# Two-layer kernel: triangular inverse in place on GpSimd, Gram with one stationary, and spreads in four row groups at once

## The chip, the cores and the metric

One core of a Trainium2 chip runs the whole program in one launch. The metric is the device time of that core in microseconds, the median over runs. TensorE (PE, with its weight loads PEld), VectorE (DVE), ScalarE (ACT) and GpSimd (POOL) run side by side and meet at semaphores; SyncE (SP) issues the plain DMAs.

## What is computed

Two transformer-like layers on x of shape 4 x 1024 x 256, all in fp32, each with adaptive shift, scale and gate per batch. Only layer 0 and the start of layer 1 touch the change.

```
layer 0, mixer:  k, q, v = short_conv(x @ W + b);  beta = sigmoid(x @ Wbeta)
                 delta rule, 16 heads of 16, per time step:
                 S += beta * k (v - k S);   o = q S
                 out = rmsnorm(o) @ Wo
layer 0, ffn:    16 routed experts of 64 channels, the best 2 per token by softmax,
                 weights renormalised; 2 shared experts of 128 channels
                 y = sum_e weight_e * (silu(x Wg_e) * (x Wu_e)) Wd_e + shared
layer 1, mixer:  complex gated linear recurrence h = a h + k v, 8 heads of 32; y = q h
layer 1, ffn:    8 experts of 1024 channels, top 2 per token
```

The delta rule is computed in chunks of 32 steps. Within a chunk it needs the inverse of a unit triangular 32 x 32 matrix for each of 16 heads x 4 batches x 4 chunks: 256 such matrices a segment, two on each of the 128 partitions.

## The kernel before, in words

**Segments.** Time is cut into eight segments of 128 steps (with 4 batches, 512 tokens). `turn(seg, rest, nxt, pre)` is called on every engine for seg = -2 to 7 and writes out each engine's order by hand. `rest` (0 to 7) is the main work of the segment, `nxt` (-1 to 6) is the delta rule of the next segment, `pre` (-2 to 5) projections, convolutions and keys of the one after. An engine runs its instructions in the order written, so a wait holds up all behind it. After the segments the experts of layer 1 run, then a last mix; the change does not touch these.

**The inverse.** At the start of a turn TensorE forms the Gram matrices (`gram`, L1959): for each head pair, batch and chunk one 32 x 32 stationary of keys Kc against beta-scaled keys of even and odd heads (EXP[0:2], 64 columns, L1966) and one stationary of scaled keys KpT against the queries (EXP[2:4], L1970). VectorE masks them into NA (L1273), SP writes NA[0] out to n_d and reads it back transposed across partitions (L584, L589), which raises n_in. Then GpSimd and VectorE take turns: for t = 1 to 31 and two halves c, GpSimd multiplies the t x t part found so far with row t (`products`, L1754, instruction L1761) and VectorE sums each row of the product into column t of Usub (`substitute`, L1187, instruction L1193), 62 of each a turn. VectorE's share is cut into pieces, `SUB_STEPS = (1, 8, 13, 16, 18, 20, 22, 24, 26)` and `SUB_LATE = 29`: one piece after each routed tile of the ffn, one before the down residuals, one after the norm, and t = 29 to 31 in the middle of layer 1's first scores, after L1479 and before L1484. sub_ok lets SP write Usub out to u_d and back into NA (L596, L601), for TensorE's `delta_rows` (L1980) late in the turn. In turn -1 the two engines do this with no other work on them.

**The expert tiles of layer 0** (TensorE from L2082, VectorE `hidden_tile`, L1328): ten tiles of 128 channels, the first two shared. A tile is four matmuls of 128x512 (gate into bank 3(i%2), up into the next bank; an fp32 matmul stands in the profile as two records). ScalarE takes silu of the gate (L809), VectorE multiplies with up (L1333), and for routed tiles with the token's routing weights (L1337). These have to stand on the right channels: VectorE makes the 16 weights of a token (L1362), TensorE turns them (`turn_weights`, L2079), VectorE copies them (L1364), and `spread(i)` (L2074) multiplies the 16 x 512 weights with a 16 x 128 selection matrix. TensorE turns and spreads tiles 2 and 3 only before tile 4; from tile 4 on, each spread stands behind its own tile. The gate of tile i waits for hid0_ok of tile i-2. Ten down matmuls a batch follow (L2108), residual and norm on VectorE (L1375 to L1392).

**Layer 1's first scores.** After twelve plane matmuls, `level(0, 0)` (L2182) scores batch by batch and puts `value_columns(b)` behind each: a bias matmul of one row (ones x b_v, L2135) that opens the bank, and two value matmuls (L2137). `level(1, 0)` needs the values taken by ScalarE. GpSimd zeroes the near scores and Hx (L1771 to L1774), multiplies for t = 29 to 31, waits for sub_ok, and zeroes score (L1780) and, after the values, the ring's score halves (L1784). VectorE's take (L1421) needs the third zeroing.

**Keys on ScalarE.** `spread_queries` (L780) copies the queries once for even and once for odd heads; then come the squares of the output (L1013), then `take_scaled_keys(k)` (L786, L788), three copies of a bank each: KpT and the two of EXP[0:2].

## Time and profile before

| | |
|---|---|
| median of 3 runs | 3630.91 us (3629.87 to 3631.79) |
| the profiled execution's own time | 3636.34 us |
| its span | 3634.4 us |
| mean granted TensorE clock | 0.817 |
| busy: TensorE, VectorE, ScalarE, GpSimd | 2796.7, 2038.2, 1163.9, 660.7 us |
| first GpSimd product of the turns -1 to 6 | 158.9, 334.7, 671.2, 1007.8, 1344.5, 1683.2, 2019.9, 2354.7 us |

The profile is one execution. A timeline row gives start, duration, engine, line, operation, output and inputs, shape and count of merged instructions, and in brackets the idle time before them with what ended it ("issue": nothing that the profile shows). The chain of waits follows the work that ended last back to the start. The granted clock is the share of TensorE's full clock, 1.00 or 0.50.

### The profile page before, as it was taken

What the parts mean: (1) busy time and instruction counts of PE and PEld (TensorE: products, weight loads), DVE (VectorE), ACT (ScalarE), POOL (GpSimd) and SP (SyncE); (2) the same over time, 40 slices, a digit from 0 to 9 for tenths busy, and PEclk for the clock granted to TensorE, in tenths of its full rate; (3) what the DMA queues carried; (4) which work ended last, traced back from release to release, by engine and by line L of the source; (5) the groups of instructions that cost most, each with busy time, mean ns of one, the idle gap of its engine ahead of it and who ended that gap; (6) DMA issues with size and microseconds to landing.
All of it is one profiled execution on the core that took longest, in us unless ns stands there. A gap on an engine that the chain in (4) does not pass through costs nothing.

```text
span 3634.4 us, 82025 instructions
## 1 busy us (share of the span) xinstructions
PE 2796.7 (77%) x35840; PEld 2039.6 (56%) x35840; DVE 2038.2 (56%) x4528; ACT 1163.9 (32%) x2276; POOL 660.7 (18%) x682
## 2 busy tenths in 40 slices
PE   3438869977896888699768978895787639999990
PEld 3225457545645664565457446645544538888880
DVE  4445785687669567955776596679336630000004
ACT  0212354145424433432353235325223512222210
POOL 0231500430051016004300510160001000000006
PEclk8667977988796879688976978796788769999995
DMA  2122201310121121112201311211110035565645
GB/s 84 24 59 42 53 8 43 78 34 24 44 58 31 42 49 46 19 43 65 48 2 55 70 31 43 48 36 25 42 41 19 2 117 193 196 198 186 200 160 166
DMA packets 230023, 247.57 MB, mean 68 GB/s; under 512 B 147361, under 2 KB 187169, under 8 KB 227361
## 3 DMA queue, kind: packets, MB, share of 16 engines
q1 hardware_dynamic: 223520, 225.54, 21.4%
q0 software_dynamic: 6144, 16.79, 1.5%
q8 instruction: 282, 4.62, 0.5%
q14 instruction: 77, 0.62, 0.1%
HBM read 196.15 MB, written 46.14 MB: 67 GB/s over the span
## 4 chain that ended last, share of the span: by engine, by line
PE 57%; DVE 21%; ACT 7%; POOL 4%; issue 4%; DMA 1%; SPq 0%; POOLq 0%; DVEq 0%
PE banks L1874 17%; PE banks L2391 7%; PE banks L2410 7%; PE banks L2108 4%; POOL arena L1761 3%; PE banks L2202 2%; PE banks L2207 2%; PE banks L1884 2%; POOL arena L1814 2%; PE banks L2182 2%; PE banks L1980 1%; PE banks L1948 1%; PE banks L2074 1%; PE banks L2021 1%; DVE arena L1523 1%
## 5 line engine op out<-in xcount | busy, mean ns | idle before, releaser
L1761 POOL TENSOR_TENSOR arena<-arena 128x1 f32<-128x1 f32 (+30 forms) x496 | 443.0, 921 | 726.4 <-DMA arena<-n_d 430.1
L1791 POOL DMA_INDIRECT h_d<-h_tok,pos_now x64 | 65.9, 1030 | 1499.0 <-DVE pos_now L1626 1482.0
L2182 PE MATMUL banks<-arena 32*32 32x64 f32 (+2 forms) x6144 | 208.7, 322 | 164.1 <-DVE arena L1526 91.7
L1193 DVE TENSOR_REDUCE arena<-arena 128x1 f32<-128x1 f32 (+30 forms) x496 | 243.1, 502 | 162.9 <-POOL arena L1761 158.3
L1874 PE MATMUL banks<-hT,ring 128*128 128x512 f32 x640 | 314.9, 645 | 8.8 <-DVE arena L1337 8.1
L2182 PE MATMUL banks<-arena,xn 32*32 32x64 f32 (+2 forms) x6144 | 193.0, 314 | 154.4 <-DVE xn L1526 117.8
L2182 PEld LDWEIGHTS banks<-arena 32*32 32x32 f32 (+2 forms) x6144 | 186.0, 196 | 204.8 <-DVE arena L1526 114.4
L1045 ACT ACTIVATE arena<-banks,arena 128x256 f32<-128x256 f32 x312 | 130.7, 470 | 457.1 <-PE banks L2391 457.1
L2391 PE MATMUL banks<-arena 128*128 128x256 f32 x1248 | 276.9, 381 | 0.0
L2410 PE MATMUL banks<-arena 128*128 128x256 f32 x1248 | 275.7, 379 | 0.0
L2182 PEld LDWEIGHTS banks<-arena,xn 32*32 32x32 f32 (+2 forms) x6144 | 177.4, 192 | 175.1 <-DVE xn L1526 128.7
L926 ACT ACTIVATE arena<-banks 32x512 f32<-32x512 f32 (+1 forms) x288 | 169.2, 588 | 290.7 <-PE banks L2182 224.4
L2391 PEld LDWEIGHTS banks<-arena 128*128 128x128 f32 x1248 | 238.3, 191 | 32.6 <-issue 0.4
L2410 PEld LDWEIGHTS banks<-arena 128*128 128x128 f32 x1248 | 234.6, 190 | 30.0
L1874 PEld LDWEIGHTS banks<-hT,ring 128*128 128x128 f32 x640 | 126.8, 205 | 187.8 <-issue 186.9
L1874 PE MATMUL banks<-arena,ring 128*128 128x512 f32 x512 | 224.0, 596 | 6.2 <-ACT arena L827 6.2
L1706 DVE COPY arena<-banks 128x512 f32<-128x512 f32 x39 | 27.0, 692 | 271.4 <-PE banks L2379 271.4
L1814 POOL DMA_INDIRECT arena<-y_d,y_at x64 | 64.6, 1009 | 609.5 <-DMA y_d<-arena 590.3
L1874 PEld LDWEIGHTS banks<-arena,ring 128*128 128x128 f32 x512 | 96.1, 190 | 128.2 <-issue 112.8
L1716 DVE TENSOR_TENSOR arena<-banks,arena 128x512 f32<-128x512 f32 x39 | 27.0, 692 | 249.4 <-PE banks L2410 249.4
L809 ACT ACTIVATE arena<-banks 128x512 f32<-128x512 f32 x80 | 47.8, 597 | 314.0 <-PE banks L1874 314.0
L2108 PE MATMUL banks<-ring,arena 128*128 128x256 f32 x640 | 140.8, 381 | 0.6 <-DVE arena L1337 0.6
(352 smaller groups left out, 5106.1 us busy)
## 6 DMA issues: line engine op xcount, KB each, us to landing
arena<-in_w_ring SPq DMA_DIRECT2D x78, 1024.0 KB, 5.1
ring<-in_w_ring SPq DMA_DIRECT2D x104, 512.0 KB, 4.5
arena<-h_d SPq DMA_DIRECT2D x39, 256.0 KB, 5.3
y_d<-arena SPq DMA_DIRECT2D x39, 256.0 KB, 5.8
n_d<-NA SPq DMA_DIRECT2D x8, 1024.0 KB, 3.8
arena<-n_d SPq DMA_DIRECT2D x16, 512.0 KB, 7.8
u_d<-arena SPq DMA_DIRECT2D x8, 1024.0 KB, 4.6
NA<-u_d SPq DMA_DIRECT2D x32, 256.0 KB, 6.5
```

The lines of the kernel that those rows point to most:

```text
L926: ins_ = act.activation(laid_, made, ACT.Copy)
L1045: ins_ = act.activation(hid1[:, i % 2, t], bank[pair][:, half * T1:(half + 1) * T1], ACT.Gelu, bias=b1[:, i % 2, t:t + 1])
L1193: dve.tensor_reduce(Usub[:, c, 0:t, t], part, AX.X, ALU.add).then_inc(*up(sub_sum, me))
L1761: pool.tensor_tensor(part, Usub[:, c, 0:t, 0:t], Nsub[:, c, t, 0:t].unsqueeze(1).to_broadcast([P, t, t]), ALU.mult)\
L1814: pool.indirect_dma_start(out=y_of[:, s % 3, k, b], out_offset=None, in_=y_d, in_offset=spot)\
L1874: i_ = mm(dst, w[:, k, cols_], rhs(src, k), start=(k == 0), stop=(k == n - 1))
L1884: i_ = mm(bank[banks[j]][:, i * D:(i + 1) * D], src[:, k, 2 * j + i, :], w[:, k, :], start=(k == 0), stop=(k == KC - 1))
L2108: i_ = mm(bank[DOWN_BANKS[b]][:, 0:D], hid0[:, i, b, :], downs[d][:, i - first, :], start=(i == 0), stop=(i == TILES0 - 1))
L2182: i_ = mm(bank[4 * hg + h][keys, b * width:(b + 1) * width], K2[rows_, r, b, keys], q, start=(r == 0), stop=(r == 1), skip_group_check=True)
L2202: mm(y, Hx[:, b, r, 2 * j:2 * j + 2].rearrange("p h j -> p (h j)"), Q3[:, 1 + r, b, :], start=(r == 0), stop=False, skip_group_check=True)
L2391: i_ = mm(bank[t // 2][:, (t % 2) * T1:(t % 2 + 1) * T1], w1[:, i % 2, t // 4, at_:at_ + P], h_cols[:, i % 2, k], start=(k == 0), stop=(k ...
L2410: i_ = mm(bank[4 + i % 2][:, j * D:(j + 1) * D], hid1[:, i % 2, t, j * P:(j + 1) * P], w2[:, i % 2, t // 4, t % 4 * D:(t % 4 + 1) * D], st ...
```

## The change

It makes five edits.

- The inverse is computed in place by outer products: Usub is loaded with the strictly triangular matrix, the diagonal is set to one, and for s = 1 to 30 the part right of s of the rows above s gains column s times row s. That is one multiply of 2 x s x (31-s) elements into sub_prod and one add of the same size, each waiting for the one before, 60 in all and a memset. In segments 0 to 6 all of it is GpSimd's, from n_in on and ahead of its zeroing; in turn -1 all of it is VectorE's. VectorE's pieces between the tiles, after the norm and within the scores are gone. Nsub and two memsets at the start are gone.
- The Gram matrices have one stationary: KpT against unscaled keys and queries together, 128 columns. The mask is turned over to suit the transposed result.
- ScalarE's EXP[0:2] come from Kc in SBUF (`spread_keys`, four copies directly behind `spread_queries`) and no longer from the banks in `take_scaled_keys`.
- The routing weights are written eight times over (comb_wide) and turned into all 128 partitions, between gate and up of tile 3; then four spreads, one in each group of 32 rows, run for tiles 2 to 5 before tile 4 and for tiles 6 to 9 before tile 7, into banks of their own. The selection matrix is loaded at four bases.
- The four value bias matmuls stand together, one in each row group, before the first scores.

```
+        def sub_operands(s):
+            n = CH - 1 - s
+            part = sub_prod[:, 0:2 * s * n].rearrange("p (c j t) -> p c j t", c=2, j=s)
+            return (part, Usub[:, :, 0:s, s:s + 1].to_broadcast([P, 2, s, n]),
+                    Usub[:, :, s:s + 1, s + 1:].to_broadcast([P, 2, s, n]), Usub[:, :, 0:s, s + 1:])
...
-                sp.dma_start(consts[:, m0:], ins["consts"][:, m1:]).then_inc(tables_in.handle, 16)
+            for r in range(0, P, ROW_TILE):
+                sp.dma_start(consts[r:r + E0, m0:], ins["consts"][0:E0, m1:]).then_inc(tables_in.handle, 16)
...
-                        sp.dma_start(Nsub[64 * half:64 * half + 64].rearrange("p c s t -> p (c s) t"), src)\
+                        sp.dma_start(Usub[64 * half:64 * half + 64].rearrange("p c s t -> p (c s) t"), src)\
...
-                    sp.wait_ge(*at(sub_ok, 1))
+                    sp.wait_ge(*(at(sub_step, SUB_STEPS) if rest else (sub_first.handle, SUB_STEPS)))
...
+                def spread_keys():
+                    for e in range(2):
+                        for k in range(KC):
+                            act.activation(EXP[:, e, k], Kc[:, k], ACT.Copy, scale=parity[:, e:e + 1])\
+                                .then_inc(*up(par_ok, me))
...
                     act.wait_ge(*at(kpT_mm, k + 1))
-                    act.activation(KpT[:, k].rearrange("p b t -> p (b t)"), bank[2 + k][:, :], ACT.Copy)
-                    for e in range(2):
-                        ins_ = act.activation(EXP[:, e, k].rearrange("p b t -> p (b t)"), bank[2 + k][:, :], ACT.Copy,
-                                              scale=parity[:, e:e + 1])
-                    ins_.then_inc(*up(kpT_ok, me))
+                    act.activation(KpT[:, k].rearrange("p b t -> p (b t)"), bank[2 + k][:, :], ACT.Copy)\
+                        .then_inc(*up(kpT_ok, me))
...
                     query_root()
                     spread_queries()
+                    spread_keys()
...
-            once(dve.tensor_scalar(causal[:, 0], near[:, :], 0.0, -1.0, ALU.is_lt, ALU.mult))
+            once(dve.tensor_scalar(causal[:, 0], near[:, :], 0.0, -1.0, ALU.is_gt, ALU.mult))
...
-                            ins_ = dve.tensor_tensor(h, h, bank[3 * (i % 2) + 2][:, :], ALU.mult)
+                            dve.wait_ge(*at(spread_mm, 1 if i in SPREADS[0] else 2))
+                            ins_ = dve.tensor_tensor(h, h, bank[SPREAD_BANK[i]][:, :], ALU.mult)
...
-                    dve.tensor_tensor(lg[:, 9], lg[:, 8], wide(sm[:, 7], E0), ALU.mult).then_inc(*up(comb_ok, me))
+                    many = [P, B, P // E0, E0]
+                    dve.tensor_tensor(comb_wide, lg[:, 8].unsqueeze(2).to_broadcast(many),
+                                      sm[:, 7].unsqueeze(2).unsqueeze(2).to_broadcast(many), ALU.mult).then_inc(*up(comb_ok, me))
...
-                        if nxt and i + 1 < TILES0:
-                            substitute(*SUB_STEPS[i - SHARED_TILES:i - SHARED_TILES + 2])
...
-                        if nxt and hg == 0:
-                            substitute(SUB_LATE, CH)
-                            dve.sem_inc(*up(sub_ok))
...
+                def substitute():
+                    pool.wait_ge(*at(n_in, n_in.nxt))
+                    pool.memset(Usub.rearrange("p c s t -> p c (s t)")[:, :, 0:CH * CH:CH + 1], 1.0)\
+                        .then_inc(*up(sub_step, me))
+                    for s in range(1, CH - 1):
+                        part, column, line, rest_ = sub_operands(s)
+                        settle()
+                        pool.tensor_tensor(part, column, line, ALU.mult).then_inc(*up(sub_step, me))
+                        settle()
+                        pool.tensor_tensor(rest_, rest_, part, ALU.add).then_inc(*up(sub_step, me))
+                    settle()
...
-                                mm(bank[GRAM_BANKS[k][g]][t, b * P:b * P + 64], Kc[p, k, b, t], EXP[p, 0:2, k, b, t],
-                                   start=True, stop=True)
-                            for g in range(4):
-                                p = slice(CH * g, CH * g + CH)
-                                i_ = mm(bank[GRAM_BANKS[k][g]][t, b * P + 64:(b + 1) * P], KpT[p, k, b, t],
-                                        EXP[p, 2:4, k, b, t], start=True, stop=True)
+                                i_ = mm(bank[GRAM_BANKS[k][g]][t, b * P:(b + 1) * P], KpT[p, k, b, t],
+                                        EXP[p, :, k, b, t], start=True, stop=True)
...
+                    def spread(tiles):
+                        for r, i in enumerate(tiles):
+                            experts = slice(ROW_TILE * r, ROW_TILE * r + E0)
+                            i_ = mm(bank[SPREAD_BANK[i]][:, :], sel[experts, i - SHARED_TILES, :],
+                                    combT[experts].rearrange("e b t -> e (b t)"), start=True, stop=True)
+                        i_.then_inc(*up(spread_mm))
...
-                        if i == SHARED_TILES + 2:
-
-                            pe.wait_ge(*at(comb_ok, 1))
-                            turn_weights(0, lg[:, 9], E0)
+                        if i == SPREADS[0][2]:
                             pe.wait_ge(*at(comb_copied, 1))
-                            spread(i - 2)
-                            spread(i - 1)
+                            spread(SPREADS[0])
...
+                        if i == SPREADS[1][1]:
+                            spread(SPREADS[1])
                         channels(bank[3 * (i % 2)][:, :], both[:, 0], c, hT).then_inc(*up(gate_mm))
-                        i_ = channels(bank[3 * (i % 2) + 1][:, :], both[:, 1], c, hT)
-                        if i < SHARED_TILES:
-                            i_.then_inc(*up(up_mm))
-                        elif i >= SHARED_TILES + 2:
-                            spread(i)
+                        if i == SPREADS[0][1]:
+                            turn_weights()
+                        channels(bank[3 * (i % 2) + 1][:, :], both[:, 1], c, hT).then_inc(*up(up_mm))
...
+                    def value_biases():
+                        for b in range(B):
+                            one = slice(ROW_TILE * b, ROW_TILE * b + 1)
+                            mm(bank[4 + b][:, :], const("ones")[one, :], row("b_v")[one, :], start=True, stop=False)
...
+                        if k == 0 and hg == 0:
+                            value_biases()
```

## Rows read from the trace of the kernel before

**Rows 1.** The chain that ended last, shares of the span by engine

```profile
PE 57%; DVE 21%; ACT 7%; POOL 4%; issue 4%; DMA 1%; SPq 0%; POOLq 0%; DVEq 0%
```

**Rows 2.** Timeline of segment 2: TensorE and VectorE in layer 0's tiles

```profile
1010.69 0.68 DVE L1364 COPY arena<-banks 16x512 f32<-16x512 f32 x1 [5.25 <-PE banks L2079]
1011.42 1.98 PE L2074 MATMUL banks<-arena,consts 16*128 16x512 f32 x4 [0.77 <-DVE arena L1364]
...
1014.23 1.96 PE L1874 MATMUL banks<-hT,ring 128*128 128x512 f32 x4 [0.83 <-DVE arena L1337]
...
1038.45 3.70 PE L1874 MATMUL banks<-hT,ring 128*128 128x512 f32 x8
...
1047.60 13.65 PE L2108 MATMUL banks<-ring,arena 128*128 128x256 f32 x62 [0.31 <-DVE arena L1337]
```

**Rows 3.** Timeline of segment 2: layer 1's first scores, all engines

```profile
1093.93 0.85 PE L2182 MATMUL banks<-arena 32*32 32x64 f32 x64 [0.78 <-ACT xn L840]
1094.71 1.12 PE L2135 MATMUL banks<-rows,consts 1*128 1x512 f32 x2
...
1108.70 1.16 DVE L1193 TENSOR_REDUCE arena<-arena 128x31 f32<-128x961 f32 x1 [1.04 <-POOL arena L1761]
...
1109.97 3.51 POOL L1780 MEMSET arena<- 128x4096 f32 x1 [1.31 <-DVEq L1482]
1110.00 1.23 DVE L1484 TENSOR_TENSOR arena<-arena 128x1024 f32<-128x1024 f32 x1
1111.26 2.50 DVE L1485 TENSOR_SCALAR arena<-arena 128x512 f32<-128x512 f32 x1
...
1117.52 1.23 DVE L1484 TENSOR_TENSOR arena<-arena 128x1024 f32<-128x1024 f32 x1
1118.78 0.43 DVE L1485 TENSOR_SCALAR arena<-arena 128x512 f32<-128x512 f32 x1
...
1110.01 2.31 PE L2182 MATMUL banks<-arena,xn 32*32 32x64 f32 x215 [1.01 <-issue]
1116.26 0.90 PE L2182 MATMUL banks<-arena,xn 32*32 32x64 f32 x41 [3.94 <-issue]
```

**Rows 4.** Timeline of segment 7, the same place, VectorE and TensorE

```profile
2779.47 1.23 DVE L1484 TENSOR_TENSOR arena<-arena 128x1024 f32<-128x1024 f32 x1 [7.17 <-PE banks L2182]
...
2786.94 1.82 PE L2182 MATMUL banks<-arena,xn 32*32 32x64 f32 x128 [2.19 <-issue]
```

**Rows 5.** A later level's timeline, and its stretch: length, busy (count), granted clock, DMA

```profile
1153.81 3.80 PE L2182 MATMUL banks<-arena 32*128 32x128 f32 x64 [2.47 <-ACT arena L926]
...
1152.00:1160.00 8.00, 4.31 (x72) 4.02 (x76) 7.79 (x19) 4.06 (x7) 0.00 (x0) 0.50 0.00 0
```

**Rows 6.** GpSimd's products by form: busy us, mean ns, idle before

```profile
L1761 POOL TENSOR_TENSOR arena<-arena 128x256 f32<-128x256 f32 x16 | 11.4, 731 | 0.0
L1761 POOL TENSOR_TENSOR arena<-arena 128x25 f32<-128x25 f32 x16 | 3.5, 242 | 0.9
L1761 POOL TENSOR_TENSOR arena<-arena 128x1 f32<-128x1 f32 x16 | 2.7, 185 | 430.1 <-DMA arena<-n_d 430.1
```

**Rows 7.** GpSimd's timeline: products of turn -1, first product of segment 2

```profile
159.43 54.34 POOL L1761 TENSOR_TENSOR arena<-arena 128x4 f32<-128x4 f32 x60 [0.19 <-DVE arena L1193]
...
1007.80 0.33 POOL L1761 TENSOR_TENSOR arena<-arena 128x1 f32<-128x1 f32 x2 [24.25 <-DMA arena<-n_d]
```

**Rows 8.** VectorE's timeline: the same add, beside a product and alone

```profile
1052.67 0.56 DVE L1376 TENSOR_TENSOR X<-X,xn 128x256 f32<-128x256 f32 x1
...
1057.49 0.42 DVE L1376 TENSOR_TENSOR X<-X,xn 128x256 f32<-128x256 f32 x1
```

**Rows 9.** The chain in order of time, end of segment 2: start, us, what

```profile
1298.67 2.44 ACT arena L780 x4
```

**Rows 10.** VectorE's masks L1273: its waits in total, one row of its timeline

```profile
  DVE NA L1273: 46.8, 13
...
1327.57 2.74 DVE L1273 TENSOR_TENSOR NA<-banks,causal 128x256 f32<-128x256 f32 x8 [3.96 <-PE banks L1970]
```

More of the change, by code:

```diff
@@ L72 @@
 CH = 32
+SUB_STEPS = 2 * (CH - 2) + 1
 ARENA = 22544
 NCH = SEG // CH
-SUB_STEPS = (1, 8, 13, 16, 18, 20, 22, 24, 26)
-SUB_LATE = 29
 DOWN_BANKS = (6, 7, 4, 5)
+SPREADS = ((2, 3, 4, 5), (6, 7, 8, 9))
+SPREAD_BANK = {2: 2, 3: 5, 4: 6, 5: 7, 6: 6, 7: 7, 8: 2, 9: 5}
+ROW_TILE = 32
 EARLY = B - 1
@@ L1065, in _ @@
             once(dve.memset(S0[:, :, :, :], 0.0))
-            once(dve.memset(Usub, 0.0))
-            once(dve.memset(Usub.rearrange("p c s t -> p c (s t)")[:, :, 0:CH * CH:CH + 1], 1.0))
             dve.wait_ge(tables_in.handle, NTAB)
@@ L1185, in flat4 @@
                     return v.rearrange("p k b h -> p (k b h)")
-                def substitute(first, end):
-                    for t in range(first, end):
-                        for c in range(2):
-                            part = sub_prod[:, c, 0:t * t].rearrange("p (j s) -> p j s", s=t)
-                            dve.wait_ge(*at(sub_mul, 2 * (t - 1) + c + 1))
-                            dve.tensor_reduce(Usub[:, c, 0:t, t], part, AX.X, ALU.add).then_inc(*up(sub_sum, me))
+                def substitute():
+                    dve.wait_ge(*at(n_in, n_in.nxt))
+                    dve.memset(Usub.rearrange("p c s t -> p c (s t)")[:, :, 0:CH * CH:CH + 1], 1.0)\
+                       .then_inc(*up(sub_first, me))
+                    for s in range(1, CH - 1):
+                        part, column, line, rest_ = sub_operands(s)
+                        settle()
+                        dve.tensor_tensor(part, column, line, ALU.mult).then_inc(*up(sub_first, me))
+                        settle()
+                        dve.tensor_tensor(rest_, rest_, part, ALU.add).then_inc(*up(sub_first, me))
                     settle()
@@ L1394, in down_norm @@
                         ins_.then_inc(*up(xn_ok, me))
-                    if nxt:
-                        substitute(SUB_STEPS[-2], SUB_STEPS[-1])
-                    down_residual(0)
-                    for b in range(1, EARLY):
+                    settle()
+                    for b in range(EARLY):
                         down_residual(b)
@@ L1798, in turn @@
                     settle()
-                counted(seg, [zeroed, sub_mul])
+                counted(seg, [zeroed, sub_step] if nxt or not rest else [zeroed])
                 pool.sem_inc(started.handle, 1)
@@ L2130, in turn @@
                             .then_inc(*up(plane_mm))
+                    def value_biases():
+                        for b in range(B):
+                            one = slice(ROW_TILE * b, ROW_TILE * b + 1)
+                            mm(bank[4 + b][:, :], const("ones")[one, :], row("b_v")[one, :], start=True, stop=False)
                     def value_columns(b):
                         w_v = slot(V_AT).rearrange("p (k c) -> p k c", k=KC)
-                        mm(bank[4 + b][:, :], const("ones")[0:1, :], row("b_v")[0:1, :], start=True, stop=False)
                         for k in range(KC):
```

71 lines of the change are left out of this document (28 added, 43 removed).

## The prediction

> **What bounds the kernel now.** I read the chain of waits first, for which engine ends a stretch: TensorE holds 57% of it, VectorE 21%, GpSimd 4% [rows 1]. An edit to GpSimd or VectorE therefore pays only where the chain passes through it. Then I read the timeline of one segment (number 2, counted from 0), stretch by stretch, since the eight segments repeat: their first GpSimd products come 335 to 339 us apart. Two of its stretches are touched, and two smaller places.
>
> The expert tiles of layer 0: after the fourth tile TensorE turns the weights, waits for VectorE's copy, spreads two tiles (1.98 us), and waits again for VectorE's multiply before the fifth starts at 1014.23. From there each tile is 3.70 us of gate and up and some 1.0 us of spread (1.98 for two), back to back: TensorE bounds it, and the reduces on VectorE between the tiles fit in. Only once, before the last down matmuls, do they cost TensorE 0.31 us [rows 2].
>
> The first scores of layer 1, from S = 1093.93: TensorE has four rounds of scores (0.8), a one-row bias matmul (1.05 to 1.12) and value matmuls (1.9), 3.75 us each, so the first group's scores are complete at S+12.1. VectorE takes them only at S+16.1 (1110.00), because the last reduces of the substitution, fed by GpSimd, sit before it. The negation L1485 then takes 2.50 us instead of 0.43, under GpSimd's memset. The second group is taken at S+23.6 [rows 3]. The last segment has no substitution: there VectorE waits 7.17 us for TensorE and takes the scores at 2779.47, so S is 2767.3; the second group's scores end at 2788.8, S+21.5, with a TensorE stall of 2.19 us inside [rows 4].
>
> **The change, part by part**, against the profiled execution (span 3634.4, time 3636.3 us, 5.4 over the median of the runs, so I take 5.4 off at the end).
>
> *Do row groups run side by side?* No row has 16-row or 1-row stationaries in four groups. The nearest has 32*128 tiles, four heads on four row groups: 64 records of 128 columns in 3.80 us at granted clock 0.50 [rows 5]. A record of 512 columns at full clock is 3.70/8 = 0.46 us, of which some 0.43 is streaming, so 128 columns at half clock are 0.21 us and 64 in a row would be 13.7 us. They ran 3.6 abreast. So four spreads cost about what one does, 1.1 us; the bounds are 1.1 and 4.2 (one after the other). I take 1.1, since the bank of each group differs as it does there.
>
> *Tiles.* Before, from the end of the fourth tile (1010.1, the copy's start less four transposes) to the end of the down matmuls (1047.60+13.65) is 51.1 us. After: four transposes 0.6 (now between the fourth tile's gate and up, so that VectorE's copy is hidden under the up matmuls of 1.7 us), one spread of four 1.15, VectorE's second multiply with its hand-overs 0.85, six tiles at 8 x 0.43 = 3.43 (20.6), a spread of four 1.15, down matmuls 80 records at 13.65/62 = 0.22 (17.6): 42.0. VectorE needs two operations of about 0.7 us a tile and has 3.4. Gain **9.1 us** in each of eight segments (8.8 in the last, which has no reduces). The wider weights (512 elements instead of 64) add some 0.5 us on VectorE before the turn; today VectorE then waits 5.25 us for it [rows 2], and 1.7 of that go as the turn moves ahead: nothing. Without that cover it would be 0.5.
>
> *Scores.* After: biases 1.1 once, rounds of 2.70. The fourth scores end at S+10.1; values end at S+11.9, the second group's scores start a second later (as now, 1.01 us after the values) at S+12.9. That level took 7.15 us in this segment (3.94 of them a stall in which TensorE waits for nothing shown) and, started at S+16.1 too, 5.4 in the last [rows 3, 4]. The longer one lies beside the substitution's transfers out and back, which now run some 35 us earlier, so I take 5.4: ready at S+18.3. VectorE has sum, negation and take of the first group (1.3, 0.4, 1.3) and two more operations of 1.25 until S+15.6, so TensorE now sets this. Its take at S+18.4 instead of S+23.6 gains **5.2 us** in seven segments; bounds 3.4 (the stall of 7.15 stays) and 7 (no stall). In the last segment S+21.6 becomes S+18.4: 3.2.
>
> *Substitution on GpSimd.* 60 instructions of 2s(31-s) elements, twice the sum over s = 1..30, that is 19,840. The product forms cost 185 ns plus 2.14 ns an element (1 element 185, 256 elements 731) [rows 6]: 11.1 + 42.5 = 53.6 us, and with an own-engine wait of about 0.1 us each, **60 us**. An add on GpSimd has no row: I bound it between VectorE's 1.05 ns and twice the product's 4.3. It starts when the transfer lands, 1007.8 [rows 7], and runs through to about 1068. First due is the zeroing that VectorE's take needs, after sum and negation, at S'+11.8; S' is 9.1 + 0.5 us earlier than now, so 1096.1, less 3.7 us for three memsets (4096 elements in all, 3.51 in one [rows 3]): 84.6 us after the start. So it costs nothing of itself. 25 elements in five rows cost only 57 ns more than one [rows 6], so short rows add at most 11 ns each, 20 us over some 1,860 rows: also covered. SP's wait for it blocks the write-out, the read-back and the next segment's X, in that order, all earlier than today; the ring loads are ahead of it in the queue.
> By the Trainium skill (GPSIMD Engine Reference, Performance pitfalls for Q7 kernels) reads whose step exceeds 8 bytes cost half as much again; no run here shows it. By that rule the substitution would take about 81 us, still inside.
>
> *Contention.* Until 1068 GpSimd now reads SBUF under the down-residuals and norms. There the add X+xn takes 0.56 beside a product and 0.42 alone [rows 8], and L1485 with a memset 2.50 instead of 0.43 [rows 3]. On the path behind the last down matmul lie one such add and two or three scalar operations: 0.1 + 2 x 0.45 (half a GpSimd instruction of 0.9) = **-1.0 us** in seven segments, bounds 0 and -3.
> By the Trainium skill (SBUF - State Buffer, Who interferes with whom) a VectorE operation in a two-port mode waits for the whole GpSimd instruction, and one with two SBUF inputs only against readers. The two rows agree with it.
>
> *First substitution (segment -1), on VectorE alone.* Nothing covers it: products until 159.43 + 54.34 = 213.8, after 0.5 us for the first, and a last reduce of 1.16, 56.1 in all, then the transfers [rows 7, 3]. Two SBUF inputs cost 0.42 for 256 elements and 1.23 for 1024 [rows 8, 3]: 0.15 + 1.055 ns each. 60 x (0.15 + 0.03 for the wait) + 20.9 = 31.8 us instead of 56.1: **+24.1**.
>
> *ScalarE.* The four key copies move in front of the squares of the output. The query copies, 2.44 us for four, are already on the chain there [rows 9]; another four delay the squares, the norm and the output projection. The shorter evacuations behind them have slack and return nothing. **-2.45 us** in seven turns (segments -1 to 5).
>
> *Gram.* Half the instructions at twice the width, the same columns. VectorE waited 46.8 us for it over 13 times, but about 4 us each of these are the second half, under which ScalarE sets the end [rows 10]. First half: **+0.5** a segment, bounds 0 and 1. The tables' smaller load at the start: nothing, bounds 0 and 1.
>
> **Sum.** Segments 0 to 5: 9.1 + 5.2 + 0.5 - 2.45 - 1.0 = 11.35, times six 68.1. Segment 6 (no key copies) 13.8. Segment 7: 8.8 + 3.2 = 12.0. Segment -1: 24.1 - 2.45 + 0.2 (Gram) = 21.9. Together 115.8: 3636.3 - 115.8 = 3520.5, and on the scale of the median **3515 us**.
>
> **Rivals.**
> A. *The row groups don't run side by side* (16 and 1 active rows, not 32): the change doesn't do what it says. Three more passes of 1.05 us in each of two spreads and in the biases: 9.45 us a segment, 75.6 in all, giving 3591. For it: no row shows such tiles abreast. Against: the 32-row ones [rows 5].
> B. *GpSimd becomes the bound, and the kernel slower.* Place: VectorE's first take of scores waits for the memsets queued behind the substitution. From 84.6 us on each us costs seven; from 84.6 + 115.8/7 = 101 us the kernel is slower than before. With twice the element rate and 0.5 us per own wait it is 11 + 85 + 30 = 126 us: 7 x 41.4 - 115.8 = +174, giving 3805. Against: the steady forms [rows 6].
> C. *Part of the gain is given back*: the stall of 7.15 us stays in each segment and contention takes 3 us: 7 x (1.8 + 2) = 26.6 less, 3542; TensorE at 1.2 instead of 2.4 GHz, as in [rows 5], for 2 us more of its work in each of the seven costs 14 more, 3556. Stall-free and without contention it is 3493.
>
> **Chances.** Forecast with C inside its range 0.84 (own range 3493 to 3556), A 0.11, B 0.04, and 0.01 that nothing measurable remains. A measurement can tell 0.2%, some 7 us. Faster 0.95, same 0.01, slower 0.04. The range 3493 to 3556 leaves out A, B and a little of C.
>
> **What would show it.** In the profile of the changed kernel: the tile rows at 3.43 us without a spread between them, two spread rows of about 1.1 us for eight records each; one bias row of 1.1 us for eight records a segment; the second group's first L1484 about 18 us after S, released by TensorE; GpSimd's substitution about 60 us and its memsets done before S; about 32 us of VectorE in segment -1; four key copies between the query copies and the squares. Wrong would be: a spread row of 4 us, VectorE idle before its take of scores with GpSimd as releaser, or segments shorter by less than 7 us.

## The result, and the profile after

The changed kernel took **3516.03 us** (median of 4 runs, 3506.78 to 3521.53) against 3631.35 (3629.87 to 3641.49) for the kernel before: ratio 0.9674, 95% interval 0.9647 to 0.9701. The forecast was 3515, range 3493 to 3556. The profiled execution took 3514.7 us with a span of 3512.8, so 121.6 us less of span where the sum was 115.8.

The chain that ended last, by engine: TensorE holds more of it than before and GpSimd half as much [rows 1].

```profile
PE 62%; DVE 21%; ACT 9%; issue 4%; POOL 2%; DMA 1%; SPq 1%; POOLq 0%; DVEq 0%; ACTq 0%
```

TensorE's timeline in the tiles of segment 2 (start, us, engine, line, operation, shapes, count, idle before and its releaser), to be held against [rows 2]:

```profile
958.93 0.60 PE L2083 MATMUL banks<-consts,arena 128*128 128x128 f32 x4
959.36 1.88 PE L1877 MATMUL banks<-hT,ring 128*128 128x512 f32 x4
961.18 1.14 PE L2075 MATMUL banks<-arena,consts 16*128 16x512 f32 x8
963.29 10.54 PE L1877 MATMUL banks<-hT,ring 128*128 128x512 f32 x24 [0.97 <-DVE arena L1355]
973.76 1.14 PE L2075 MATMUL banks<-arena,consts 16*128 16x512 f32 x8
974.83 10.57 PE L1877 MATMUL banks<-hT,ring 128*128 128x512 f32 x24
985.23 17.43 PE L2109 MATMUL banks<-ring,arena 128*128 128x256 f32 x80
```

The turn (L2083) lies between gate and up, eight spread records (four spreads) take 1.14 us, and three tiles of 24 records 10.54 to 10.57 without a spread between them. From the end of the fourth tile's up matmuls (961.24) to the last down matmul's end (1002.66) are 41.4 us; with the four transposes, which now lie inside that tile, 42.0, against 51.1: gain 9.1.

Layer 1's first scores, TensorE and then VectorE, against [rows 3]:

```profile
1037.12 1.14 PE L2137 MATMUL banks<-rows,consts 1*128 1x512 f32 x8 [0.78 <-ACT xn L854]
1038.19 0.85 PE L2190 MATMUL banks<-arena 32*32 32x64 f32 x64
1038.98 1.98 PE L2143 MATMUL banks<-ring,arena 128*128 128x512 f32 x4
...
1050.07 2.31 PE L2190 MATMUL banks<-arena,xn 32*32 32x64 f32 x215 [1.01 <-issue]
1054.49 0.78 PE L2190 MATMUL banks<-arena,xn 32*32 32x64 f32 x41 [2.12 <-issue]
...
1047.25 1.22 DVE L1493 TENSOR_TENSOR arena<-arena 128x1024 f32<-128x1024 f32 x1 [5.09 <-PE banks L2190]
1048.51 0.43 DVE L1494 TENSOR_SCALAR arena<-arena 128x512 f32<-128x512 f32 x1
```

Four biases take 1.14 us together. VectorE's sum of the first group (L1493) now waits 5.09 us for TensorE at S'+10.1, where it stood behind the substitution before; the negation is back to 0.43 us. The second group's scores start at S'+12.95, their stall is 2.12 us and not 3.94, and layer 1's level work begins at 1058.3, S'+21.2, against S+26.5 before.

GpSimd's and VectorE's substitutions, each from its first instruction, against [rows 6, 7]:

```profile
301.91 0.21 POOL L1764 MEMSET arena<- 128x64 f32 x1 [299.84 <-DMA arena<-n_d]
302.20 0.29 POOL L1769 TENSOR_TENSOR arena<-arena 128x60 f32<-128x60 f32 x1
...
148.31 0.11 DVE L1203 MEMSET arena<- 128x64 f32 x1 [8.08 <-DMA arena<-n_d]
148.46 0.22 DVE L1208 TENSOR_TENSOR arena<-arena 128x60 f32<-128x60 f32 x1
```

GpSimd's ends at 356.2 (54.3 us), its three zeroings at 359.8, while the scores start at 383. VectorE's in turn -1 ends at 180.7 (32.4 us).

**The ledger.** The first masks of each turn (L1273 before, L1290 after) cut the execution: turn -1 ends 30.5 us earlier (the sum had 21.9), segments 0 to 5 give 13.0, 8.0, 12.4, 13.6, 12.8 and 10.5, together 70.3 (68.1), and what follows 20.8 (25.8).

### The profile page after: what moved, and what is told of

Read it like the earlier page. It is cut to its first block, busy times and chain, and to the rows that moved or that the text cites. A ratio compares the mean times of both kernels' runs of the same rounds, so it can differ in the third digit from the quotient of the medians.

```text
span 3512.8 us, 77489 instructions
## 1 busy us (share of the span) xinstructions
PE 2680.6 (76%) x33792; PEld 1991.0 (57%) x33792; DVE 1819.2 (52%) x4091; ACT 1165.3 (33%) x2276; POOL 565.4 (16%) x613
## 4 chain that ended last, share of the span: by engine, by line
PE 62%; DVE 21%; ACT 9%; issue 4%; POOL 2%; DMA 1%; SPq 1%; POOLq 0%; DVEq 0%; ACTq 0%
PE banks L1877 19%; PE banks L2399 8%; PE banks L2418 8%; PE banks L2190 3%; PE banks L2109 3%; PE banks L2210 2%; PE banks L2215 2%; POOL arena L1817 2%; PE banks L2143 2%; PE banks L1951 1%; PE banks L1887 1%; PE banks L1979 1%; PE banks L2020 1%; DVE arena L1532 1%; DVE arena L1518 1%
## 5 line engine op out<-in xcount | busy, mean ns | idle before, releaser
L1877 PE MATMUL banks<-hT,ring 128*128 128x512 f32 x640 | 298.5, 624 | 7.8 <-DVE arena L1355 7.8
L1877 PE MATMUL banks<-arena,ring 128*128 128x512 f32 x512 | 224.0, 595 | 6.2 <-ACT arena L841 6.2
L1877 PEld LDWEIGHTS banks<-hT,ring 128*128 128x128 f32 x640 | 125.6, 201 | 168.2 <-issue 168.2
L1771 POOL TENSOR_TENSOR arena<-arena 128x60 f32<-128x60 f32 (+14 forms) x210 | 180.5, 859 | 16.5
L1769 POOL TENSOR_TENSOR arena<-arena 128x60 f32<-128x60 f32 (+14 forms) x210 | 167.0, 795 | 16.5
L1877 PEld LDWEIGHTS banks<-arena,ring 128*128 128x128 f32 x512 | 96.0, 190 | 129.3 <-issue 112.9
L2109 PEld LDWEIGHTS banks<-ring,arena 128*128 128x128 f32 x640 | 121.6, 190 | 19.9 <-issue 3.8
```

Source lines behind the costliest of these rows:

```text
L1769: pool.tensor_tensor(part, column, line, ALU.mult).then_inc(*up(sub_step, me))
L1771: pool.tensor_tensor(rest_, rest_, part, ALU.add).then_inc(*up(sub_step, me))
L1877: i_ = mm(dst, w[:, k, cols_], rhs(src, k), start=(k == 0), stop=(k == n - 1))
L2109: i_ = mm(bank[DOWN_BANKS[b]][:, 0:D], hid0[:, i, b, :], downs[d][:, i - first, :], start=(i == 0), stop=(i == TILES0 - 1))
```

## The experiments

The experiments were run in three later sets, recorded on chips numbered 0, 8 and 8; the number of the first profiles' chip is not on record. In these sets the kernel before takes 3670.39, 3670.28 and 3662.86 us (single runs 3656 to 3680). The changed kernel was run in the first two: 3530.58 (3527.36 to 3535.26) and 3529.55 (3525.77 to 3534.99), where I had expected 3516 and 3510 to 3535; ratio 0.9623 (0.96 to 0.9645) and 0.9611 (0.9596 to 0.9627). Each experiment is held against the changed kernel of its own set, those of the third set (products thrice, ten steps) against that of the second.

**The changed kernel again** (no edit), first set and second set.

> The changed kernel again, as the base of this set. 3516 us, ratio to the kernel before 0.967 to 0.969; nothing tells theories apart here.

> The changed kernel once more, as the base for the runs beside it, since chips differ by some tenths of a per cent between calls: 3510 to 3535 us. In its trace ScalarE's last evacuations to the next masks take either 10.7 us (as in the first profile) or 13.9 (as in the second); no theory of mine says which.

Both times the stretch from the start of ScalarE's last evacuation to the first masks is 13.9 us in turns 2 to 6 (14.2 in turn 1), where the first profile has 10.7 (11.1); in turn 0 it is 10.7 to 11.2 in all three. The tiles are the same. What differs is the Gram. TensorE's timeline of this place in turn 3, first in the second set, then in the first profile:

```profile
1257.96 1.01 PE L1969 MATMUL banks<-arena 32*32 32x128 f32 x44
1259.28 0.42 PE L1969 MATMUL banks<-arena 32*32 32x128 f32 x5 [0.31 <-issue]
...
1262.94 0.43 PE L1969 MATMUL banks<-arena 32*32 32x128 f32 x2 [1.02 <-issue]
```

```profile
1250.96 2.20 PE L1969 MATMUL banks<-arena 32*32 32x128 f32 x128
```

In the first profile 128 short matmuls run in one piece of 2.20 us; in the later ones, after 42 to 47 of them, TensorE stops every five or so for 0.3 to 1.0 us while it waits for nothing that the profile shows. Both chip numbers show it, so whether the chip makes the difference is not shown.

**The kernel before, in the third set** (no edit, profiled).

> The kernel before, profiled on the chip of the later runs, where it takes 3670 us instead of 3631 while the changed kernel takes 3530 instead of 3516. My theory: TensorE's stalls between many short instructions (idle that the profile gives as issue) are longer on this chip, and the Gram of before has twice as many instructions as that after, so its stretch from ScalarE's last evacuations to the masks, 10.3 to 12.6 us in the first profile, is 15 to 17 us here, the 3 us of the changed kernel's Gram twice over. Rival (a clock or DMA difference that acts everywhere): every stage is longer by about 1%.

3674.22 us (one run). From the evacuations to the masks are 17.2, 15.3, 17.4, 15.6, 15.7 and 17.2 us in turns 1 to 6, as my theory had it, while tiles (50.5 to 50.8 us from the copy of the weights) and norm to scores (32.7) are as in the first profile, not 1% longer. The kernel before had stops in its first profile too, of 1.5 to 3.4 us in turns 0 to 6 and 5.1 in turn -1, but none of the short ones after some 44 matmuls. VectorE's waits for the Gram (total, count, longest) in the kernel before in the first profile, the same in the third set, the changed kernel in the first profile, in the second set:

```profile
DVE NA L1273 <- PE banks L1970: 46.8, 13, 10.3
```

```profile
DVE NA L1273 <- PE banks L1970: 76.1, 15, 10.4
```

```profile
DVE NA L1290 <- PE banks L1969: 33.7, 9, 8.0
```

```profile
DVE NA L1290 <- PE banks L1969: 52.7, 15, 8.0
```

The Gram's edit takes 13.1 us of waits away in the first profiles and 23.4 in the later ones. That is 10 of the 25 us by which the change gains more there (140 against 115). Some 9 more lie in the scores: in five of the eight segments the kernel before of the third set needs 28.3 us from S to the level, not 26.5, which I did not trace further.

**One row group.** All spreads and biases come from row group 0.

```
-                            experts = slice(ROW_TILE * r, ROW_TILE * r + E0)
+                            experts = slice(0, E0)
...
-                            one = slice(ROW_TILE * b, ROW_TILE * b + 1)
+                            one = slice(0, 1)
```

> The changed kernel, but all four spreads of a set and all four bias rows come from row group 0, so that they can't run side by side; the work and its order stay. My theory (the gain in the tiles and half of that in the scores is concurrency of the row groups): three more passes of about 1.05 us in each of two spread sets and in the biases. The set rows of eight records go from 1.14 us to about 4.2; each segment is 6 to 9.4 us longer, the kernel 50 to 75 us slower than the changed one, some 3567 to 3591 us. Rival (the gain came from the order alone: turn ahead of the up matmuls, one wait less; the row groups only look abreast in the records): no difference, 3516.

3618.68 us (3614.08 to 3622.79, 4 runs): 88.1 more than the changed kernel beside it. So concurrency is shown: in the tiles 6.8 of the 9.1 us go with it, and the order alone is worth at most the rest. But 88 is above my range. TensorE's timeline, tiles and then scores of segment 2, and two stretches (length, busy and count of TensorE, weight loads, VectorE, ScalarE and GpSimd, granted clock, DMA share, GB/s):

```profile
988.73 3.69 PE L2075 MATMUL banks<-arena,consts 16*128 16x512 f32 x8
993.37 12.23 PE L1877 MATMUL banks<-hT,ring 128*128 128x512 f32 x24 [0.94 <-DVE arena L1355]
1005.54 3.70 PE L2075 MATMUL banks<-arena,consts 16*128 16x512 f32 x8
1009.16 10.57 PE L1877 MATMUL banks<-hT,ring 128*128 128x512 f32 x24
...
1069.47 4.54 PE L2137 MATMUL banks<-rows,consts 1*128 1x512 f32 x8 [0.78 <-ACT xn L854]
...
1074.96 3.78 PE L2143 MATMUL banks<-ring,arena 128*128 128x512 f32 x4
```

```profile
993.30:997.00 3.70, 3.63 (x5) 1.65 (x6) 1.21 (x2) 0.13 (x1) 3.45 (x4) 0.55 0.01 2
...
1074.90:1078.70 3.80, 3.80 (x19) 1.20 (x8) 0.00 (x0) 0.00 (x0) 0.00 (x0) 0.50 0.00 0
```

The passes themselves cost 2.55 us a set and 3.40 in the biases, 8.5 a segment, inside my range. The rest goes with the clock: after 3.7 us of back-to-back matmuls on 16 rows and a wait of 0.94, the next tile ran at a granted clock of 0.55 (12.23 us for three tiles, not 10.54), and after 4.5 us on one row the first values ran at 0.50 (3.78 us, not 1.98). Behind the second set, with no wait after it, the clock stayed. By stretches a segment is 6.8 us longer in the tiles, 1.4 from there to the scores (the biases' 3.4, less 1.4 since the matmuls behind the norm took 5.18 us here and 6.61 beside it, and 0.5 ahead of them) and 2.3 in the scores: 10.5, and eight times that is 84.

**Biases apart.**

```
                     def value_columns(b):
+                        mm(bank[4 + b][:, :], const("ones")[0:1, :], row("b_v")[0:1, :], start=True, stop=False)
...
-                        if k == 0 and hg == 0:
-                            value_biases()
```

> The changed kernel with the value biases back in front of each value matmul, one at a time. My theory (they are on TensorE's path to the second group's scores, which sets VectorE's take): each bias 1.05 us, four of them instead of one pass of 1.14, so the take of the second group 3.1 us later in each segment, 22 to 25 us slower than the changed kernel. Rival (VectorE's own chain of sum, negation and take bounds it once the substitution has left): 0 to 8 us slower.

3553.83 us (3546.67 to 3560.58, 4 runs): 24.3 more, 3.0 a segment. VectorE's two sums, here and in the changed kernel beside it, segment 2:

```profile
1053.52 1.23 DVE L1493 TENSOR_TENSOR arena<-arena 128x1024 f32<-128x1024 f32 x1 [7.18 <-PE banks L2189]
...
1062.56 1.23 DVE L1493 TENSOR_TENSOR arena<-arena 128x1024 f32<-128x1024 f32 x1 [3.62 <-PE banks L2189]
```

```profile
1053.74 1.23 DVE L1493 TENSOR_TENSOR arena<-arena 128x1024 f32<-128x1024 f32 x1 [5.09 <-PE banks L2190]
...
1061.64 1.23 DVE L1493 TENSOR_TENSOR arena<-arena 128x1024 f32<-128x1024 f32 x1 [2.47 <-PE banks L2190]
```

Both sums still wait for TensorE in either kernel: with the substitution gone, TensorE's order is the bound and each of its microseconds counts. Of the gain in the scores 3.0 us are the biases'. The rest, 2.2 to 2.5, is left for the substitution's departure and the shorter stall together; no run parts these two.

**Gram in halves.** The stationary keys stay, but are loaded twice, with 64 moving columns each.

```
-                                i_ = mm(bank[GRAM_BANKS[k][g]][t, b * P:(b + 1) * P], KpT[p, k, b, t],
-                                        EXP[p, :, k, b, t], start=True, stop=True)
+                                mm(bank[GRAM_BANKS[k][g]][t, b * P:b * P + 64], KpT[p, k, b, t],
+                                   EXP[p, 0:2, k, b, t], start=True, stop=True)
...
+                                i_ = mm(bank[GRAM_BANKS[k][g]][t, b * P + 64:(b + 1) * P], KpT[p, k, b, t],
+                                        EXP[p, 2:4, k, b, t], start=True, stop=True)
```

> The changed kernel with the Gram's stationary keys used twice with 64 moving columns each instead of once with 128. My reading after the result (keys stationary gave about 8 us in the turn before segment 0, where nothing covers the Gram, and 0.5 us in each of seven others): turn -1 later by up to 8 us, each other turn by 0.5, together 5 to 12 us slower than the changed kernel. Rival (the 8 us of turn -1 came from elsewhere, such as the evacuations): 0 to 4 us slower.

3542.14 us (3540.52 to 3557.57, 4 runs): 12.6 more, just beyond my range, and with another split. Segments 0 to 5 are 1.4 to 3.2 us longer up to the next first masks and not 0.5, together 12.8, since the stops come with the count of instructions, and another 4.8 from the first masks to the second. In turn -1 the second masks come 12.5 us after the last evacuation's end instead of 6.2, as in the first profiles (12.6 before, 6.3 after). This is more than the time shows. What comes back lies behind the masks: 8.3 us up to the fourth tile's end and 5.4 between the second take of scores and the squares. Half of the 8.3 is a change of releaser ahead of the router's matmuls (segment 2, here and in the changed kernel beside it):

```profile
961.17 2.00 PE L2064 MATMUL banks<-w_router,hT 128*128 128x16 f32 x16 [0.82 <-DVE NA L1290]
```

```profile
947.54 3.57 PE L2060 MATMUL banks<-w_router,hT 128*128 128x16 f32 x16 [1.62 <-ACT hT L723]
```

With the Gram in halves the second masks release them; in the changed kernel ScalarE's hT does, 1.6 us after these masks begin instead of 0.7 to 1.1, so 0.7 us a segment of the shorter Gram is not on the path. VectorE's waits for the Gram in halves:

```profile
DVE NA L1290 <- PE banks L1973: 76.6, 15, 10.6
```

These are the 76.1 us of the kernel before: the number of instructions alone makes the Gram's part of the waits.

**Key copies behind the squares.**

```
                     spread_queries()
-                    spread_keys()
...
                     take_scaled_keys(0)
+                    spread_keys(0)
...
                     take_scaled_keys(1)
+                    spread_keys(1)
```

> The changed kernel with ScalarE's four key copies moved behind the squares of the output: two after each of the first and second evacuation of scaled keys. My theory (they delay squares, norm and output projection by 2.45 us in each of seven turns): the stretch from delta_rows to the squares shorter by 2.4 us, the kernel faster by about 17 us than the changed one, 3499 us. Rival (the copies fill a wait that is there anyway, or the evacuations behind them become late): no gain, 3512 to 3520.

3516.88 us (3513.12 to 3525.48, 5 runs), 13.7 less than the changed kernel beside it: the four copies do cost about 2 us a turn.

**Query and key copies behind the squares**, as two, three and three; the last three behind the evacuations for the output projection.

```
-                    spread_queries()
-                    spread_keys()
...
                     take_scaled_keys(0)
+                    spread_some(0, 2)
...
                     take_scaled_keys(1)
+                    spread_some(2, 5)
...
+                if pre:
+                    spread_some(5, 8)
```

> As the run before, but the four query copies too are moved behind the squares (two, three and three copies in the gaps between ScalarE's later evacuations). My theory: another 2.44 us per turn off the chain ahead of the squares, of which part comes back before the Gram, since all eight copies must be done for it: 17 to 34 us faster than the changed kernel, 3482 to 3499, and at most as fast as the run before if the Gram has to wait. Rival (ScalarE's later evacuations set the Gram's start): slower than the run before by up to 2.4 us in each of seven turns.

**3509.22 us** (3501.3 to 3513.82, 5 runs), ratio to the kernel before 0.956 (0.9536 to 0.9583): 21.4 less than the changed kernel, the fastest of all. ScalarE's timeline at the end of segment 2:

```profile
1221.76 1.09 ACT L1019 ACTIVATE arena<-banks 128x512 f32<-128x512 f32 x2 [1.64 <-PE banks L2015]
1222.77 0.60 ACT L796 ACTIVATE arena<-banks 128x512 f32<-128x512 f32 x1
1223.27 1.32 ACT L791 ACTIVATE arena<-Qc,parity 128x512 f32<-128x512 f32 x2
1224.87 0.26 ACT L1026 ACTIVATE o_sum<-o_sum 128x64 f32<-128x64 f32 x1 [0.28 <-DVE o_sum L1299]
...
1229.25 1.93 ACT L791 ACTIVATE arena<-arena,parity 128x512 f32<-128x512 f32 x3
```

The squares (L1019) now wait 1.64 us for TensorE, so ScalarE no longer sets them. The first two copies fill a wait: before the root behind them (L1026) 0.28 us are left, where the changed kernel has 1.55. Of the query copies' 2.44 us a turn 1.1 were gained (7.7 us over seven turns).

**GpSimd's products twice, and thrice** (the second with `range(3)`).

```
-                        settle()
-                        pool.tensor_tensor(part, column, line, ALU.mult).then_inc(*up(sub_step, me))
+                        for _ in range(2):
+                            settle()
+                            pool.tensor_tensor(part, column, line, ALU.mult).then_inc(*up(sub_step, me))
```

> The changed kernel with each of GpSimd's 30 products of the substitution made twice: 54.3 us become about 82 to 86 (products are 1.04 us for 480 elements, sum 27 to 31). My slack of 84.6 us after its start: no change in time, within 4 us, as GpSimd's zeroings end just when VectorE's take needs them. If the slack is smaller than I worked out (rival: contention on more of the path, or the transfers out and back then late for the next segment) the kernel is slower by 7 us for every us that is missing, 10 to 60 us.

> The changed kernel with each of GpSimd's products made three times: about 54.3 + 2 x 29 = 112 us from the transfer's landing, 28 beyond my slack of 84.6. Rival B of the prediction at its real price: VectorE's first take of scores waits for GpSimd's zeroings about 28 us in each of seven segments, 196 us, and with the contention seen for two products another 10 to 35: 3730 to 3765 us, slower than the kernel before. If the slack is larger than I worked out, or the wait overlaps work that is late anyway: 3600 to 3700.

Twice: 84 to 87 us on GpSimd and 3547.34 us (3539.8 to 3554.99, 4 runs), 17.8 more, where I expected 4 at most. No wait of VectorE for GpSimd has appeared; its sum in segment 3 still waits 5.09 us for TensorE. What grew are VectorE's own rows. All 32 adds of X+xn (L1392), busy time and mean ns, in the kernel that stops after ten steps (below), the changed one and this one:

```profile
L1392 DVE TENSOR_TENSOR X<-X,xn 128x256 f32<-128x256 f32 x32 | 13.6, 425 | 1.1
```

```profile
L1392 DVE TENSOR_TENSOR X<-X,xn 128x256 f32<-128x256 f32 x32 | 20.4, 638 | 1.1
```

```profile
L1392 DVE TENSOR_TENSOR X<-X,xn 128x256 f32<-128x256 f32 x32 | 24.5, 767 | 1.1
```

So the rival written for this run holds, contention on more of the path: 2.5 us a segment by the time. Two places show in the segments 0 to 5: from the last down matmul to the matmuls behind the norm 1.4 us more a segment, and in two of them the negation (L1494) under GpSimd's zeroing, 2.88 and 5.36 us instead of 0.43. The rest was not placed.

Thrice: some 114 us on GpSimd and 3701.78 us (3699.47 to 3705.39, 4 runs), 172 more than the changed kernel of the second set (180 when the kernels before of the two sets are made equal), ratio to the kernel before 1.0105 (1.0076 to 1.0134). That is less than the 3730 to 3765 that I expected, but rival B's wait exists:

```profile
DVE h_tok L1433 <- POOL arena L1783: 155.8, 7, 24.2
```

22.3 us a segment in seven: the slack was 114 - 22.3, some 92 us, and not 84.6.

**Ten steps.** GpSimd's substitution stops after step 10, and the inverse is set to zero; the rest of it, and with it the delta rule's update, is left out.

```
-                    for s in range(1, CH - 1):
+                    for s in range(1, 11):
...
+                    settle()
+                    pool.memset(Usub, 0.0).then_inc(*up(sub_step, me))
```

> The changed kernel with GpSimd's substitution stopped after step 10 of 30, and the inverse then set to zero: steps 11 to 30 and with them the state update of every chunk are left out, the rest of the work stays. GpSimd is then done some 30 us earlier, before VectorE's down residuals. My theory (contention costs 0.8 us a segment on the adds and scalings of the norm): VectorE's add on X back to 0.42 us, three scalings back to about 1.1, each of seven segments 0.8 to 2 us shorter, 6 to 14 us faster than the changed kernel. Rival (they are slow for another reason): no difference.

3528.15 us (3516.78 to 3536.14, 4 runs), 1.4 less than the changed kernel of the second set, or 6 more when the kernels before are made equal: no gain that the time can tell. The add fell to 425 ns and the scalings from 699 to 492 ns as expected. But from the last down matmul to the matmuls behind the norm the mean of segments 0 to 6 fell only from 5.40 to 4.87 us, which is what the kernel before has: contention of the changed kernel costs the path 0.5 us a segment. My size was too high.

**The read-back's buffer moved** (in the kernel before).

```
-        Nsub, _ = carve(14000, [P, 2, CH, CH])
+        Nsub, _ = carve(13984, [P, 2, CH, CH])
```

> The kernel before with the buffer that the negated Gram rows are read back into moved by 16 floats, from an offset of 64 beyond a multiple of 128 bytes to a multiple. Theory (the read-back became 2 us shorter with the change, 7.8 to 5.8 us from issue to landing, since it now lands in the inverse's buffer, which is aligned so): 5.8 us here too, and turn -1 about 2 us shorter. Rival (it is shorter since the blocks written before it or the traffic beside it changed): 7.8 us as in the kernel before.

The DMA issues (KB each, median us from issue to landing) of the kernel before in this set, of this one, and of the changed kernel:

```profile
arena<-n_d SPq DMA_DIRECT2D x16, 512.0 KB, 7.7
```

```profile
arena<-n_d SPq DMA_DIRECT2D x16, 512.0 KB, 6.2
```

```profile
arena<-n_d SPq DMA_DIRECT2D x16, 512.0 KB, 5.8
```

In turn -1 the first product follows the write-out's issue by 12.3 us (141.68 to 153.95), by 14.6 without the edit. So the buffer's start sets 2.3 us of this way, by one profile each. The time, 3663.46 us in one run, can't tell 2 us.

## Why the prediction was right, point by point

In the segments 0 to 5 the profiles before and after differ by 11.7 us each in the mean, where the sum had 11.35 (parts rounded): tiles 9.2 (9.1), scores 5.5 (5.2), Gram up to the router's matmuls 0.9 (0.5), router and first four tiles -0.25 (no term), last down matmul to the norm's matmuls -0.6 (contention, -1.0), those matmuls -0.7 (no term), second take of scores to the squares -2.2 (key copies, -2.45). The total is right because the large terms are; below them some ground was wrong, and turn -1 and the last stretch missed by 8.6 and 5.0 us with opposite signs, which is luck.

- **Tiles, 9.1 us a segment: right**, and for the reason given. The set of four costs 1.14 us (1.1 taken); in one row group it costs 3.7, and with the biases there too the kernel loses 88 us.
- **Scores, 5.2 us: right in size** (5.2 to 5.8 in segments 0 to 5), **by a row that was read wrongly**. I took the shorter stall, worth 1.8 of the 5.2 us, from the last segment, where the second group's scores seemed to end at S+21.5 after 5.4 us [rows 4]. They do not end there. The next row of TensorE in the kernel before is:

```profile
2790.69 0.43 PE L2182 MATMUL banks<-arena,xn 32*32 32x64 f32 x5 [1.93 <-issue]
```

  So that level took 7.8 us, more than the 7.15 of segment 2, and VectorE's sum came at S+24.0. The changed kernel has 7.7 us and S'+20.8 there: the gain of 3.2 is as summed, with both ends 2.4 us later. In segments 0 to 6 the level took 4.6 to 7.15 us in the kernel before, segment 2 the longest, and 4.7 to 5.4 in the changed one (the stall from 3.94 to 2.12 us in segment 2). My reason was that the substitution's transfers no longer run beside it; but the last segment has none in either kernel and keeps the long stall, which speaks against it. Why the long ones are gone elsewhere stays open, and that 5.4 came true is luck. What the change took away for certain is VectorE's own chain, which put its sum at S+23.6 in all seven segments of the kernel before, without a wait in [rows 3].
- **Substitution on GpSimd costs nothing: right.** 54.3 us against 60; an add (1160 ns for 480 elements) costs little more than a product (1044). From 60 to 480 elements a product grows by (1044 - 300)/420 = 1.8 ns an element, less than the 2.14 of [rows 6], though the column operand steps 128 bytes. The rule of the Trainium skill (GPSIMD Engine Reference, Performance pitfalls for Q7 kernels) would have given half as much again. But its remedy speaks of the inner step of the access pattern, and here the inner step of the column operand is 0 (it is repeated) and the 128 bytes are the step outside it. So this trace shows only that such an outer step does not cost half as much again; it doesn't test the rule.
- **Slack 84.6 us: some 92 with the products thrice, about 90 in the changed kernel.** The step that is too small is the way from the landing to S': 82.1 us in the mean of seven segments instead of 76.5. The transfer lands some 2 us sooner after the masks, the way from the masks to the fourth tile's end grew by 1.9, and that from the last down matmul to S' by 1.5. The rest is VectorE's own rows, which are later beside a longer substitution.
- **Contention, -1.0 a segment: too much.** The adds grew as said, but 0.5 to 0.6 reached the path. Beside it stood a loss that I had only in rival C, the clock of the matmuls behind the norm (64 records of L1877 on hT and w_in, total and mean, before and after):

```profile
L1874 PE MATMUL banks<-hT,w_in 128*128 128x512 f32 x64 | 43.5, 843 | 13.1 <-ACT hT L820 13.1
```

```profile
L1877 PE MATMUL banks<-hT,w_in 128*128 128x512 f32 x64 | 50.5, 963 | 12.1 <-ACT hT L834 12.1
```

  In segment 2 they had a granted clock of 0.57 where it was 0.69. That is 0.9 us a segment over all eight; with GpSimd long done it is the same (50.1), so it is not contention. Why the clock stands lower there was not tried. The two wrong sizes nearly cancel, 1.4 against 1.0.
- **Key copies, -2.45 a turn: right in kind.** Moving them gave 13.7 us, 2.0 a turn. The part not seen is that the query copies, which the change leaves in place, hold the same place and can go as well.
- **Gram, +0.5 a segment and 0.2 in turn -1: the step that failed.** In segments 0 to 5 the second masks come 1.6 us sooner after the evacuations; 0.7 of that is lost again, since the router's matmuls then wait for ScalarE, and 0.9 remains. In turn -1 they come 6.3 us after the last evacuation's end instead of 12.6: 6.3 us and not 0.2, of which 4.5 are stops of TensorE without a releaser (5.1 us before, 0.5 after). I gave that turn half a segment's gain, though nothing there covers the Gram's second half; [rows 10] says only for the late turns that ScalarE sets it. The whole turn: 1.9 us from an earlier start of ScalarE's copies (121.2 against 123.2; 120.9 to 125.1 in later profiles of both kernels, so this is the spread of executions), 6.3 Gram, 2.5 from the write-out to the first substitution (2.3 of them the buffer's start, which had no term), 23.7 substitution and -3.9 for the rest, where I had -2.45 for the key copies: 30.5 against 21.9.
- **Last stretch: 20.8 instead of 25.8.** The matmuls behind the norm lose 1.5 and 1.3 us in segments 6 and 7, the way from the masks to the fourth tile's end 2.8 in segment 6, and 1.1 and 0.9 more go behind the scores of the two segments, which was not traced.
- **Substitution on VectorE: 32.4 against 31.8.** Right.

## What to carry to other kernels

Matmuls with few rows belong side by side in different row groups and banks, in sets, and the wait for their input goes between matmuls that don't need it: here this cost one pass instead of four and kept the clock. An engine that is given covered work needs two checks and not one: when its result is due, and which rows of the other engines slow down beside it until then. Before a first or last turn gets the term of a middle one, ask which of its covers are missing there. And when a merged row is taken for the end of some work, count its instructions: 123 + 128 were read as all of 256.

## What the runs showed of the hardware that I had not expected

- TensorE's clock stood lower behind passes with few rows, though TensorE was busy all through them: 3.7 us of gapless matmuls on 16 rows with a 0.94 us wait behind them, and 4.5 us on one row, were followed by full-size matmuls at a granted clock of 0.55 and 0.50. The same work in four row groups, 1.14 us, was followed by 1.00, and so was a second set of 3.7 us with no wait behind it.
- Strings of short matmuls can stop without a releaser. In the later profiles of the changed kernel this began after 42 to 47 instructions, 0.3 to 1.0 us every five or so, 18 us in all; in the first profile it was 1.3 us in all. With it the gain of halving the Gram's instructions went from 13 to 23 us of waits. What decides between the two is open.
- A transfer of 512 KB into SBUF landed in 7.7 us when its buffer's offset was 64 bytes past a multiple of 128, and in 6.2 when it was one, in one profile each.
